# Cross-attention scores as plain fp32 products in two row tiles, with keys projected twice and rotated out of PSUM

## What is computed

```python
q = (lat @ Wq).reshape(b, n, HEADS, DHEAD).transpose(0, 2, 1, 3)
kv = ctx @ Wkv
k, v = jnp.split(kv, 2, axis=-1)
k = apply_rope(k, cos[None, None], sin[None, None])   # [x1*cos - x2*sin, x2*cos + x1*sin]
attn = jnp.einsum('bhnd,bhsd->bhns', q, k) * scale
attn = jnp.clip(attn, -11.0, 11.0)
attn = jax.nn.softmax(attn, axis=-1)
out = jnp.einsum('bhns,bhsd->bhnd', attn, v)
return out.transpose(0, 2, 1, 3).reshape(b, n, INNER) @ Wo + bo
```

## Time and profile before

| | us |
|---|---|
| median of three runs | 1328.63 |
| the profiled execution | 1330.58 |
| its span, first to last instruction | 1328.9 |
| TensorE busy | 1046.6 (79%) |
| VectorE busy | 896.4 (67%) |
| ScalarE busy | 672.7 (51%) |
| GpSimd busy | 644.2 (48%) |
| mean granted TensorE clock | 0.898 of full |

### The profile page before, as it was taken

How to read it: one execution, slowest core, us unless ns; L and a number is a source line. 1 busy time by engine, 2 the same in 40 slices (tenths; PEclk the granted TensorE clock), 3 DMA queues, 4 the chain that set the end, 5 groups by cost and what they waited for, 6 DMA issues and landing times.

```text
span 1328.9 us, 18554 instructions
## 1 busy us (share of the span) xinstructions
PE 1046.6 (79%) x6579; PEld 679.0 (51%) x6579; DVE 896.4 (67%) x2076; ACT 672.7 (51%) x1863; POOL 644.2 (48%) x617
## 2 busy tenths in 40 slices
PE   5667978898788889888888978888854999998321
PEld 3354555465455546545554654555543665664321
DVE  3348776968787796878779687877976000444598
ACT  3746846764684686468468646844520123332000
POOL 1137656746765674676567467656841000111032
PEclk9769998999999999999999999999985679998655
DMA  6000000000000000000000000000000000000301
GB/s 167 1 4 9 1 1 12 1 1 5 8 1 1 13 1 1 5 9 1 1 13 1 1 1 1 1 1 1 1 17 0 0 1 2 7 8 5 32 16 32
DMA packets 56810, 12.76 MB, mean 10 GB/s; under 512 B 40318, under 2 KB 56462, under 8 KB 56590
## 3 DMA queue, kind: packets, MB, share of 16 engines
q1 hardware_dynamic: 56718, 11.58, 4.1%
HBM read 9.46 MB, written 2.12 MB: 9 GB/s over the span
## 4 chain that ended last, share of the span: by engine, by line
PE 40%; DVE 34%; ACT 10%; POOL 10%; issue 4%; DMA 1%; SPq 0%; POOLq 0%; DVEq 0%; ACTq 0%
PE bank_d L1672 5%; PE score_banks L1379 5%; PE score_banks L1731 4%; PE bank_a L1360 4%; DVE qm_s L1025 4%; DVE stats L887 3%; PE score_banks L1381 3%; DVE k_sin L1015 3%; PE score_banks L1380 3%; DVE kr_s L1019 3%; DVE prob L1079 3%; PE score_banks L1402 2%; PE out_bank L1624 2%; DVE o_rec L1071 2%; POOL psum L584 2%
## 5 line engine op out<-in xcount | busy, mean ns | idle before, releaser
L505 POOL TENSOR_TENSOR var_eps<-mv,epsilons 128x2 f32<-128x2 f32 (+2 forms) x64 | 12.7, 199 | 405.9 <-DVE mv L890 405.9
L765 ACT ACTIVATE prob<-score_banks 128x512 f32<-128x512 f32 x256 | 152.5, 596 | 104.3 <-PE score_banks L1381 101.8
L584 POOL TENSOR_TENSOR psum<-psum,prob 128x512 f32<-128x512 f32 x64 | 109.2, 1707 | 121.4 <-DVE prob L1079 120.9
L1379 PE MATMUL score_banks<-qm_s,kr_s 128*128 128x512 f32 x256 | 139.1, 543 | 29.9 <-DVE kr_s L1019 29.0
L1079 DVE TENSOR_SCALAR prob<-prob 128x1024 f32<-128x1024 f32 x128 | 111.1, 868 | 50.0 <-ACT prob L765 49.8
L1559 PE MATMUL out_bank<-prob,v 128*64 128x256 f32 x896 | 115.2, 389 | 2.4 <-DVE on L1072 2.3
L1025 DVE SCALAR_TENSOR_TENSOR qm_s<-q_raw,pair_mask,qm_s 128x256 fp32r<-128x256 f32 x128 | 80.7, 671 | 52.1 <-ACT qm_s L733 52.1
L582 POOL TENSOR_TENSOR psum<-prob 128x512 f32<-128x512 f32 x64 | 92.0, 1437 | 38.3 <-DVE prob L1079 38.3
L1380 PE MATMUL score_banks<-qm_s,kr_s 128*128 128x512 f32 x256 | 108.7, 425 | 0.0
L1381 PE MATMUL score_banks<-qm_s,kr_s 128*128 128x512 f32 x256 | 108.1, 422 | 0.0
L692 ACT ACTIVATE prob<-prob,neg_max 128x128 f32<-128x128 f32 (+1 forms) x256 | 106.2, 421 | 0.0
(11 more groups left out here) (336 smaller groups left out, 2627.0 us busy)
## 6 DMA issues: line engine op xcount, KB each, us to landing
cb<-in_ctx_dram SPq DMA_DIRECT2D x8, 256.0 KB, 2.8
bias_mask<-bias_scratch SPq DMA_DIRECT2D x1, 1536.0 KB, 7.3
xb<-in_x_dram SPq DMA_DIRECT2D x8, 128.0 KB, 2.1
prob<-in_L_xattn_Wkv_dram SPq DMA_DIRECT2D x1, 1024.0 KB, 6.6
att_scratch<-on SPq DMA_DIRECT2D x16, 64.0 KB, 3.1
prob<-att_scratch SPq DMA_DIRECT2D x2, 512.0 KB, 4.0
out_dram<-v SPq DMA_DIRECT2D x4, 256.0 KB, 2.3
prob<-in_L_xattn_Wq_dram SPq DMA_DIRECT2D x1, 512.0 KB, 7.4
```

The source lines that it names most:

```text
L584: link(g.tensor_tensor(psum[:, p % 2, :], psum[:, p % 2, :], pp[:, 2, :], ALU.add))
L765: s.activation(prob[:, p % 2, kb, :], sc[:, kb % 2, :], ACT.Exp, scale=DH ** -0.5).then_inc(exp_done, 1)
L1379: mm(out_ap, a_high, b_low, start=True, stop=False, **kw)
```

## The change

Scores: a unit is now two context blocks of a pair. Each head's 64 rows of keys and of queries are multiplied by themselves, as plain fp32, head 0 in the upper 64 rows of the array and head 1 in the lower 64, into two banks. A unit is four products of 64 rows by 128 by 256; both score banks belong to one unit, and ScalarE empties them with one exponential of 1024 columns.

Keys: they are projected twice, with Wk (job "keys a") and with Wk's halves of each head swapped (job "keys b", `wkx_s`). VectorE multiplies the first from PSUM by the cosine and the second by the signed sine, and GpSimd adds the two into `kr`. The split of keys and queries in high and low parts goes, and with it the masked copies.

Order: values, sum and `attended` of a pair stand in the next pair, also over the boundary of a batch; the output product of a batch stands in pair 0 of the next, its normalization in pair 1. The two layer norms of slot 39 are spread over slots 39, 40 and 42, and the transposes of the latents move from slot 42 to 43.

```diff
-            def keys(job, prep, after=True):
-                act.wait_ge(p_full, job)
-                if after:
-                    act.wait_ge(kr_ready, prep - 1)
-                s.activation(k_raw[:, :], bank_p, ACT.Identity).then_inc(p_free, 1)
-            def keys_high(prep, buf):
-                act.wait_ge(ksum_ready, prep)
-                s.activation(kr_s[:, buf, 0, :], k_raw[:, :], ACT.Identity).then_inc(kr_high, 1)
...
-                        s.activation(prob[:, p % 2, kb, :], sc[:, kb % 2, :], ACT.Exp,
+                        s.activation(prob[:, p % 2, 2 * u:2 * u + 2, :].rearrange("p k (h q) -> p h k q", h=2),
+                                     sc[:, 0:2, :].rearrange("p h (k q) -> p h k q", k=2), ACT.Exp,
                                      scale=DH ** -0.5).then_inc(exp_done, 1)
...
-            def keys_sin(job, prep):
-                dve.wait_ge(p_free, job)
-                w.tensor_tensor(k_sin[0:DH, :], k_raw[DH:P, :], sin_t[DH:P, :], ALU.mult)
-                w.tensor_tensor(k_sin[DH:P, :], k_raw[0:DH, :], sin_t[0:DH, :], ALU.mult).then_inc(ksin_ready, 1)
-            def keys_low(prep, buf):
...
-            def queries_low(job, buf):
...
+            def keys(job, key, part):
+                dve.wait_ge(p_full, job)
+                if part == "a":
+                    if key >= 1:
+                        dve.wait_ge(kr_ready, key)
+                    w.tensor_tensor(k_cos[:, :], bank_p, cos_t[:, :], ALU.mult).then_inc(p_free, 1)
+                else:
+                    w.tensor_tensor(k_sin[:, :], bank_p, sin_t[:, :], ALU.mult).then_inc(p_free, 1)
...
+            def rotate(key):
+                pool.wait_ge(p_free, KEYS_DONE[key])
+                g.tensor_tensor(kr[:, key % 2, :], k_cos[:, :], k_sin[:, :], ALU.add).then_inc(kr_ready, 1)
...
+                    def unit(u):
+                        if u == 0:
+                            pe.wait_ge(kr_ready, pair + 1)
+                            pe.wait_ge(p_free, QUERIES_DONE[pair])
+                        if 2 * pair + u >= 1:
+                            pe.wait_ge(exp_done, 2 * pair + u)
+                        for k in range(2):
+                            kb = 2 * u + k
+                            for h in range(2):
+                                rows_of = slice(DH * h, DH * (h + 1))
+                                last = mm(sc[:, h, k * T:(k + 1) * T], kr[rows_of, p % 2, kb * P:(kb + 1) * P],
+                                          qh[rows_of, p % 2, :], start=True, stop=True, skip_group_check=True)
+                        last.then_inc(unit_full, 1)
...
+                    unit(0)
+                    slots(0, 1)
+                    if pair >= 1:
+                        values_of(pair - 1)
+                        sum_of(pair - 1)
+                    slots(1, 2)
+                    unit(1)
+                    values_job(0)
+                    keys_job("a")
+                    slots(2, 3)
+                    if "queries" in target:
...
+                        prep_queries(JOB[b, p, "queries"], target["queries"])
+                    slots(3, 4)
+                    keys_job("b")
+                    values_job(1)
+                    slots(4, 5)
+                    if p == 0 and b >= 1:
+                        output(b - 1)
+                    slots(5, 6)
```

More of the change, by code:

```diff
@@ L72, with prep_targets, number_jobs @@
 SETUP_D = 3
[L74 to L91, removed]
+def prep_targets(p, last):
+    target = {}
+    if p % 2 == 1 and not (last and p == PAIRS - 1):
+        target["values 0"] = (p + 1) // 2 % (PAIRS // 2)
+    if p + 2 < PAIRS or not last:
+        target["keys a"] = (p + 2) % PAIRS
+    if p + 1 < PAIRS or not last:
+        target["queries"] = (p + 1) % PAIRS
+    if p + 2 < PAIRS or not last:
+        target["keys b"] = (p + 2) % PAIRS
+    if "values 0" in target:
+        target["values 1"] = target["values 0"]
+    return target
+FIRST_JOBS = [("keys a", 0), ("keys b", 0), ("values 0", 0), ("values 1", 0), ("queries", 0), ("keys a", 1),
+              ("keys b", 1)]
+def number_jobs():
+    at, count = {}, len(FIRST_JOBS)
+    done = {"queries": [FIRST_JOBS.index(("queries", 0)) + 1],
+            "keys b": [FIRST_JOBS.index(("keys b", k)) + 1 for k in range(2)]}
+    for b in range(B):
+        for p in range(PAIRS):
+            for kind in prep_targets(p, b == B - 1):
+                at[b, p, kind] = count
+                count += 1
+                if kind in done:
+                    done[kind].append(count)
+    return at, count, done["queries"], done["keys b"]
+JOB, ALL_JOBS, QUERIES_DONE, KEYS_DONE = number_jobs()
+SELF_NORMS = 5
+UNITS = 2 * PAIRS
 HALVES = 2 * PAIRS
-SELF_DVE_LINKS, DVE_LINKS, LAST_DVE_LINKS = 6, 16, 10
-SELF_POOL_LINKS, POOL_LINKS, LAST_POOL_LINKS = 13, 38, 23
 Z_FIRST = 512
@@ L1219, in _ @@
             for b in range(0, B):
[L1220 to L1221 removed]
+                late = n(b, EARLY_NORMS, B * SELF_NORMS + 8)
                 job = 10 + b * EARLY_D
@@ new lines, in _, with output @@
+            for done, (kind, target) in enumerate(FIRST_JOBS):
+                if kind[:4] == "keys":
+                    prep_keys(done, target, kind[-1])
+                if kind[:6] == "values":
+                    prep_values(done, target, int(kind[-1]))
+                if kind == "queries":
+                    pe.wait_ge(lat_split, 1)
+                    prep_queries(done, target)
+            def output(b):
+                for p in range(PAIRS):
+                    if p >= PAIRS - 2:
+                        pe.wait_ge(on_ready, n(b, PAIRS, p + 1))
```

441 lines of the change are left out of this document (173 added, 268 removed).

## The result

The changed kernel is slower: 1414.14 us, the median of four runs (1400.40 to 1420.27), against 1329.03 for the kernel before on the same chip. The ratio is 1.063 (95% interval 1.055 to 1.071). The forecast was 1315, with a range up to 1354. The profile is of the execution of 1411.65 us.

The account below looks back on a forecast made before the run. TensorE bounds the kernel, VectorE close behind. Setup +5.1, seven batches -24.5, first batch's output -3.6, last batch +7.9 make -15.1 from 1330.6; 1313.5 at the median plus 1.5 for hand-overs gives 1315 us, range 1276 to 1354.

Parts of the forecast that it names:

- the 1.0 taken: TensorE's time for a new score unit, its two row tiles running beside each other: 1.0 us, 2.0 in a pair.
- The setup: Ahead of the first unit: seven jobs in a row on one bank, +4.1 us, and one more weight copy, +1.0.
- The bank of projections: Chain late next: keys a, queries and keys b each wait for one bank to be emptied; two pairs take 20.6 us.
- Pairs 4 and 5: Middle of a batch: pair 4 set by ScalarE, 14.7 us, pair 5 16.1; sum 30.8 us, 31.6 before.
- The walk: Step-by-step timing of pairs from the earlier trace's durations: a batch 112.6 us, the last batch 85.3.
- rival B: Slower by the one bank, hand-overs meeting busy queues: 0.5 us in each of 56 pairs, 1343; decides from 0.27; chance 0.29.
- 1.8 us for the reciprocal ahead of the second clamp in pairs 1 to 3: In pairs 0 to 3, reciprocal and slot 1's row maxima make the second clamp late: 1.8 us of 56.5.
- C: Much faster: slots fill the waits, a batch comes down to TensorE's work, 105 us; total 1260; chance 0.13.
- D: Row tiles don't run beside each other: 1.7 us more in each of 64 pairs, about +100, 1415; chance 0.05.
- pairs 0 to 3 and the last batch would be slower: Sign: pairs 0 to 3 take 56.5 us for 51.9, the last batch 85.3 for 77.4; otherwise the forecast is wrong.
- batches of 112.6: Sign in the trace after: a batch takes 112.6 us, 3.5 less than before.
- faster by four or more beyond the moved output: Sign: pairs 6 and 7 take 25.3 us for 32.7, of which 3.6 only moved.

Follow-up runs that it names:

- one_tile: Changed kernel with both heads' score products taken from rows 0 to 63, so all four of a unit lie in one row tile; 1514.16 us, one run.
- fill_all: Changed kernel plus small unused TensorE products in its waits, in pairs 1, 2, 3, 7 of seven batches and 1 to 6 of the last; 1364.23 us.
- late_att: Changed kernel with VectorE's reciprocal and scaling moved behind the second clamp and keys a's cosine product in every pair; 1397.80 us.
- fill_att2: fill_all with the reciprocal and scaling moved behind the second clamp and cosine product in pair 2 of the first seven batches alone; 1344.59 us.
- twobank_att2: Changed kernel with queries and values also using a second projection bank in some pairs, and the reciprocal moved behind the second clamp in pair 2; 1272.29 us.
- heads: Changed kernel with a score unit's two loops exchanged: both products of the upper row tile, then both of the lower; 1399.34 us.

## Why the prediction was wrong

**What held.** A unit starts 1.07 us ahead of the next work (604.33 to 605.40), for the 1.0 taken; the exponential takes 1023 ns, the products out of the bank 687 and 688:

```profile
L753 ACT ACTIVATE prob<-score_banks 128x1024 f32<-128x1024 f32 x128 | 131.0, 1023 | 186.6 <-PE score_banks L1547 186.2
L996 DVE TENSOR_TENSOR k_sin<-score_banks,sin_t 128x512 f32<-128x512 f32 x64 | 44.0, 688 | 93.6 <-PE score_banks L1342 93.6
L994 DVE TENSOR_TENSOR k_cos<-score_banks,cos_t 128x512 f32<-128x512 f32 x64 | 43.9, 687 | 22.0 <-PE score_banks L1342 22.0
```

The Trainium skill (TensorEngine Tiling (Array Packing), Key Properties) says that tiles run in parallel; one_tile against the changed kernel agrees, with 1.99 us for 1.14. The setup cost 3.7 us for 5.1. The bank of projections was the right name for what is late: in the middle batch it accounts for 15.8 of TensorE's 20.5 us of idle time. Pairs 4 and 5 took 31.5 for 30.8.

**The step that failed: the clock.** The walk took every duration of TensorE from the earlier trace rows, at 2.4 GHz, and let pauses cost their own length. By stretch the miss is 72.8 us in the seven batches, 16.1 in the last, 8.4 behind it, and -1.4 ahead of the first unit. The prediction named the danger in one half sentence, "a last batch with TensorE idle a third of the time, whose clock may fall", gave it no term, and gave rival B 0.5 us a pair for hand-overs instead. The earlier trace rows held the warning: 0.97 and 0.98 in the batches against 0.74 behind them, in the part where one step waits for another. fill_all gives it a size: 50 us of the total by the medians, and in the profiles 22.6 us in the seven batches and 15.6 in the last, net of what the fill itself costs and with the clock of the seven still at 0.96. In the last batch it is all of the miss, 101.4 for a forecast of 85.3 and 85.8 with the clock held.

**The mis-sized term: 1.8 us for the reciprocal ahead of the second clamp in pairs 1 to 3.** The mechanism stands as put; in pair 2 alone it costs 2.4 us a batch with the clock held (15.7 to 13.3). In the timeline slot 13's row maxima and a norm's measure stand ahead of it (620.79 to 622.84), and the clamp behind it took 1.68 us for the 0.69 that the walk gives it; how much each of them is worth was not measured. Together with late_att it says that neither place of the reciprocal is right for all pairs.

**What is left.** The clock is not the whole loss: fill_all is still 33 us above the kernel before. fill_att2 has the clock (0.98) and pair 2 nearly put right: in its middle batch 56.9, 31.5 and 26.8 us for the three groups of pairs, for 56.5, 30.8 and 25.3 forecast; 1344.6 for 1315 in all. The rest is 23 us in seven batches, of which the fill's own products are a part that was not measured, and 7 behind the last one, which are no effect of the change.

**The rivals.** B's mechanism was right and its price far too small: 1343 for 1414. Its point, 0.27 us a pair, was passed. Most of the miss is the clock that the pauses take along and pair 2; but the 23 us left in fill_att2 are 0.4 us for each of 56 pairs, so hand-overs alone may have passed it too, and the fill's own products keep that open. C needed the slots to fill the waits; twobank_att2 comes near its batch of 105 (105.6 in the middle one), but only with a second bank. D had the number, 1415, by a mechanism that one_tile refutes; that the time is D's is chance. The range was too narrow because no rival priced a batch at a lower clock: at 0.81 that was worth 16 us in the last batch alone.

**The signs.** That pairs 0 to 3 and the last batch would be slower held (62.6 us for 51.9, 101.4 for 77.4); "batches of 112.6" failed and pointed beyond B's 117. The sign for pairs 6 and 7, "faster by four or more beyond the moved output", failed as well: 29.1 us for 32.7, and 3.6 of that is the output. Pair 6 took 11.4 of the 11.6 forecast; pair 7 took 17.7 for 13.7, at a clock of 0.72, and 14.5 in fill_all at 0.95.

## What to carry to other kernels

A pause on TensorE is not worth its own length alone. Where a change makes TensorE wait more often, take the walk a second time with its products at half speed in the pairs with long pauses, and let that second result set the upper end. Before a second projection or a longer chain is laid on one PSUM bank, look for a bank that is free in part of the program: here the same change went from 6% slower to 4% faster than the kernel before, by a second bank and one moved reciprocal. And before a few microseconds of a total are put down to an edit, compare the stretches that it touches: the code that no edit touched differed by up to 11 us between executions.

## What the runs showed of the hardware

The code behind the last batch is the same in all kernels, but took 346.3 to 348.9 us in eight of the profiles (the kernel before among them) and 354.8 to 357.6 in the other six. Here are 25 us of the recurrence at the same distance behind the last batch, of the changed kernel and of heads:

```profile
1215.00:1240.00 25.00, 24.83 (x196) 17.59 (x194) 8.72 (x26) 7.12 (x39) 2.92 (x8) 0.72 0.08 7
```

```profile
1218.80:1243.80 25.00, 24.84 (x242) 15.09 (x241) 10.44 (x32) 8.50 (x47) 3.65 (x10) 1.00 0.08 7
```

196 records for 242 in the same time: in some executions the clock falls there for a while though TensorE is busy throughout, in others not. Both groups have kernels of every kind, so the 8.4 us behind the last batch are hardly the change's. Each kernel has one profile, so how often a kernel falls in either group is not known, nor why the clock falls there.

heads was a surprise too: products that follow each other in one row tile, then in the other, took no longer than products in turns, though one_tile shows that one tile alone is slower. By the records above, two begin together in heads as well, though in its program four records of one tile stand ahead of the first of the other. The Trainium skill (TensorE: Matmul & The Clock Gate, the table at its head) says that TensorE's queue has a partial reorder window, by which weight loads are pulled ahead of products. No run here shows whether that is what lets the second tile begin early.
